# Eight semaphores instead of four for a stream of scatters, and a constant column in place of a comparison, in a four-layer graph kernel

## The reference, cut to what matters

```python
x = _layernorm(x + _L0(x, src, dst))                     # message: x[src]
x = _layernorm(x + _L1(x, edge_attr_32, W, ...))         # message: relu(x[src] + edge_attr), then two linear maps
x = _layernorm(x + _L2(x, src, dst, edge_weight, W))     # gathers x[dst] * weight, sums by src
x = _layernorm(x + _L3(x, edge_index, w_src, w_tgt, b))  # gathers x[src] * gate * norm, sums by dst
# in _L3:
deg = jax.ops.segment_sum(jnp.ones(E), src)              # how many edges leave each node
```

## Time and profile before

| what | value |
|---|---|
| median of three runs | 8055.8 us (8040.68 to 8060.42) |
| time of the profiled execution | 8085.47 us |
| its span, first to last instruction | 8083.7 us |
| granted TensorE clock, mean | 0.835 |
| busy: PE / DVE / ACT / POOL | 72% / 86% / 49% / 51% |
| sort and first scatters, about | 0 to 1380 us |
| first layer, about | 1390 to 2580 us |
| second layer, about | 2610 to 4803 us |
| third layer, about | 4926 to 6577 us |
| fourth layer, about | 6686 to 7948 us |

### The profile page before, as it was taken

How to read it: one execution, slowest core, us unless ns; L and a number is a source line. 1 busy time by engine, 2 the same in 40 slices (tenths; PEclk the granted TensorE clock), 3 DMA queues, 4 the chain that set the end, 5 groups by cost and what they waited for, 6 DMA issues and landing times. The chain is left out here.

```text
span 8083.7 us, 287895 instructions
## 1 busy us (share of the span) xinstructions
PE 5818.8 (72%) x120824; PEld 5437.1 (67%) x120824; DVE 6912.9 (86%) x8082; ACT 3967.8 (49%) x5752; POOL 4145.9 (51%) x3710
## 2 busy tenths in 40 slices
PE   5767775888885666666653255777777749999995
PEld 4666664777775666666653255777777749999995
DVE  8999998999996999998974347889889888999994
ACT  2333332444442555555542226889999853333331
POOL 4555777777777777777777730000000005666662
PEclk8888887999997888888776666777778769999996
DMA  7866212777773777777764324666666626666661
GB/s 127 148 119 119 42 27 59 174 175 175 175 175 95 210 207 205 208 209 205 210 173 120 91 78 158 204 207 212 213 209 216 203 99 215 201 204 201 202 202 43
DMA packets 1123439, 1316.76 MB, mean 163 GB/s; under 512 B 581317, under 2 KB 869253, under 8 KB 1122183
## 3 DMA queue, kind: packets, MB, share of 16 engines
q1 hardware_dynamic: 768861, 739.56, 33.3%
q10 hardware_dynamic: 250536, 508.89, 22.0%
q0 software_dynamic: 103168, 54.68, 2.8%
HBM read 902.26 MB, written 400.43 MB: 161 GB/s over the span
## 5 line engine op out<-in xcount | busy, mean ns | idle before, releaser
L675 POOL DMA_INDIRECT slot_table<-recs,idx_now x3224 | 3280.9, 1018 | 1349.9 <-issue 879.0
L1547 PE MATMUL banks<-hot_d,msg 128*96 128x256 bf16 x10192 | 1547.4, 307 | 1044.5 <-DVE msg L1032 836.2
L1547 PEld LDWEIGHTS banks<-hot_d,msg 128*96 128x96 bf16 x10192 | 1262.2, 136 | 1185.3 <-DVE msg L1032 874.0
L686 POOL TENSOR_TENSOR msg_z<-left,msg_z 128x448 bf16<-128x448 f32 x364 | 816.7, 2244 | 2387.6 <-ACT msg_z L1389 2387.6
L950 DVE TENSOR_TENSOR hot_d<-lodl,banks 128x2560 bf16<-128x2560 bf16 (+1 forms) x884 | 1487.6, 1683 | 0.0
L1356 ACT CAST far_now<-hot_td 128x3584 fp8e4<-128x3584 bf16 x364 | 1154.7, 3172 | 34.7 <-DVE hot_td L969 33.3
L1320 ACT CAST near_now<-hot_t 128x1792 fp8e4<-128x1792 bf16 x364 | 613.9, 1686 | 1035.5 <-DMA source_marks<-near_now 596.2
L1601 PE MATMUL banks<-x_win,hot_td 128*128 128x32 bf16 x30576 | 883.4, 182 | 222.9 <-issue 208.5
L1601 PEld LDWEIGHTS banks<-x_win,hot_td 128*128 128x128 bf16 x30576 | 831.6, 100 | 249.0 <-issue 234.4
L1289 ACT CAST msg<-banks 128x480 bf16<-128x480 f32 (+1 forms) x1040 | 522.1, 554 | 631.5 <-PE banks L1547 593.6
L961 DVE TENSOR_TENSOR hot_t<-lo_bc,banks 128x1280 bf16<-128x1280 bf16 (+1 forms) x884 | 807.9, 914 | 10.1 <-DMA lo_bc<-row_table 10.0
(11 more groups left out here) (190 smaller groups left out, 9974.9 us busy)
## 6 DMA issues: line engine op xcount, KB each, us to landing
lo_bc<-row_table ACTq DMA_DIRECT2D x364, 448.0 KB
dl_bc<-row_table SPq DMA_DIRECT2D x364, 448.0 KB, 4.6
target_marks<-far_now SPq DMA_DIRECT2D x364, 448.0 KB, 3.1
dl_bc<-target_marks SPq DMA_DIRECT2D x364, 448.0 KB, 4.2
lo_bc<-row_table ACTq DMA_DIRECT2D x468, 320.0 KB
slot_table<-zeros SPq DMA_DIRECT2D x52, 1617.0 KB, 10.8
rec_in<-slot_table ACTq DMA_DIRECT2D x364, 231.0 KB
source_marks<-near_now ACTq DMA_DIRECT2D x364, 224.0 KB
```

The source lines that it names most:

```text
L675: pool.indirect_dma_start(out=slot_dram[c.number], out_offset=bass.IndirectOffsetOnAxis(ap=idx_now[:, c.slot, g:g + 1], axis=0), in_=recs[ ...
L686: pool.tensor_tensor(msg3[:, blk.slot, :, 2 * D:3 * D], left3[:, blk.slot], msg3[:, blk.slot, :, D:2 * D], ALU.subtract).then_inc(msg_made ...
L1547: mm = t.matmul(banks[0:3 * D, 6 + blk.par, 0:WIN], rows[:, blk.slot, g, :], hot[:, blk.slot, g // 2, :, g % 2], start=(blk.b == 0 and g = ...
```

## The change

`LANES` goes from 4 to 8. By it there are eight semaphores `scattered[k]`; a scatter waits for the one eight places before it; `landed` counts each semaphore's share of the 62; `wait_scattered` waits on eight; and the condition at L673, `g - (LANES - 1) in (16, 32, 48)`, holds at places 23, 39 and 55 instead of 19, 35 and 51.

In the third layer column 32 of `msg_z` is set to 1.0 once, in both slots, at the start of `sum_targets`, with a drain behind it. The comparison of L1073 goes, and PE waits for one increment of `hot_d_made[2]` per block, not two.

```diff
-LANES = 4
+LANES = 8
@@ in sum_targets, on DVE
+                v.memset(msg_z[:, :, :, D], 1.0)
+                dve.drain()
                 first = Block(0, 0)
                 make_hot_td(2, first)
@@ in make_hot_s, on DVE
                                 ).then_inc(hot_d_made[2], 1)
-                v.tensor_scalar(msg_z[:, blk.slot, :, D],
-                                lodl[:, bass.ds(blk.chunk, 1), HB + blk.h0:HB + blk.h0 + BG].rearrange(
-                                    "p c g -> p (c g)"), 0.5, None, ALU.is_ge).then_inc(hot_d_made[2], 1)
@@ in sum_targets, on PE
-                    pe.wait_ge(hot_d_made[2], 2 * blk.number + 2)
+                    pe.wait_ge(hot_d_made[2], blk.number + 1)
                     pe.wait_ge(msg_made[2], blk.number + 1)
```

## The result

The changed kernel takes 7748.8 us (median of 4 runs, 7745.6 to 7758.0) against 8055.8 us: a ratio of 0.9624, 95% interval 0.9607 to 0.9641, or 307 us less. The forecast was 7750 us. The profiled execution took 7748.5 us, its span is 7746.7 us. It lies on the median of its kernel, where that of before lay 30 us above its own; so the two traces differ by 337 us and the medians by 307 us. Where those 30 us were I can't say.

What follows compares the result with a forecast made beforehand. POOL's scatter stream was taken to bound the second layer's end; 314 - 5 + 10 = 319 us off gave 7766 us for the profiled execution, 7737 us from the median, so 7750 us, range 7705 to 7870 us.

Steps and rivals of the forecast that it cites:

- ACT's waits for the stream: Second layer: ACT waits for scatters before its cast, 8 times, 374.4 us, once per chunk for the last 8 chunks.
- POOL's gain: Scatter stream: of 463.6 us of waits 347.5 us go; last scatter starts at 4403 us instead of 4739.8.
- The 11 us of longer scatters: POOL: some 160 more scatters fall into the sort, each 0.07 us longer, a loss of 11 us.
- Rival 2: Scatters before 900 us: the DMA queue limits them, those waits all stay; 7921 us, chance 0.08.
- My 10 to 11 us: Scatters before 900 us: time a late scatter takes to land, nearly covered by eight in flight, 10.2 us.
- What is late next: End of second layer: its own pace binds, 23 us to spare; last product at 4486 us, a gain of 314 us.
- a sign of being wrong: Second layer's last chunks: if ACT still waits for scatters there, the prediction is wrong.
- My 0.7 us gained per block: End of second layer: steps without scatters beside them gain 0.7 us each, 13 us for 18 steps, taken as cancelled.
- Four more waits on ACT: Second layer: `wait_scattered` has four more waits, 51 times on ACT; costs 0 to 12 us, taken as 5 us.
- The third layer: Dropping DVE's comparison saves at most 29 us; the share of blocks where PE waits, 126 of 330, arrives: 10 us.
- the 15 us for the profiled execution: Whole time: profiled execution lay 29.7 us above the median; forecast of 7750 us set between 7766 and 7737 us.
- rival 4: POOL: scatter instructions themselves take longer with eight in flight; time about 8450 us if one in four took 1.9 us, chance 0.04.

Runs made afterwards that it cites:

- lanes8: Kernel before with eight semaphores instead of four, comparison per block kept; on a chip with the long sort: 11351.6 us, ratio to before 0.9962.
- late4: Kernel before with the constant column, four semaphores, and POOL starting scatters only when all 52 chunks are ranked: 9357.1 us, ratio 1.1437.
- late8: Kernel before with the constant column, eight semaphores, and POOL starting scatters only when all 52 chunks are ranked: 9144.6 us, ratio 1.1192.

## Why the prediction was right

- **What bounds it.** ACT's waits for the stream in the earlier trace rows were read rightly but for one: of the 8 waits and 374.4 us, 39.9 us stand before the layer's first cast, at 2614 us. It is there with 39.7 us in the changed kernel and with 40.0 us in lanes8, where the scatters had long ended, so it isn't a wait for them. Seven chunks waited, 334 us. The sum doesn't use this number. The last product came 60.4 us after the last scatter, as it was 59.6 us before, and 60 us in both late kernels. That the waits for scatters pass to the time one for one while the second layer waits is shown by late4 and late8.
- **POOL's gain.** Expected: 347.5 us less 11, last scatter at 4403 us. Measured 4413.2 us, 10 us later. The waits that stay are 62.9 - 89 x 0.30 = 36 us; I had taken none. Two terms, 27 us together, made up for most of it. The 11 us of longer scatters did not come: all 3224 are busy for 3280.9 us before and 3281.4 us after. And the idle time beyond 0.30 us that the view puts down to issue fell by 16 us, from 879.0 - 2813 x 0.30 = 35 to 944.5 - 3085 x 0.30 = 19 us; nothing in my sum held that.
- **Rival 2 and the rule behind it.** Refuted wherever it was measured. Before 900 us the waits fell from 257.3 to 54.1 us, and on the other chips from over 300 to 86 to 101 us with eight and to 12 to 40 us with ten. The Trainium skill ("DMA: Bandwidth & Descriptors", Queues, rings and completion order) says that an engine drains one packet of about 9 to 17 descriptors from a queue before it turns to the next. That more in flight gain nothing was my step from it, and these runs don't bear it out. More in flight do not make a scatter land later at worst, either: from its start to the end of the wait for it, it took up to 13.1 us with four and up to 13.8 us with eight in the traces of before and after, and up to 14.3 and 14.2 us on the other chips. The longest with four (before, timeline of POOL; the second waits for the first):

```profile
814.40 2.48 POOL L675 DMA_INDIRECT slot_table<-recs,idx_now  x1 [0.30 <-issue]
...
827.52 0.96 POOL L675 DMA_INDIRECT slot_table<-recs,idx_now  x1 [6.83 <-DMA slot_table<-recs,idx_now]
```

  The longest with eight (the changed kernel, chain of work, start and duration):

```profile
642.08 13.52 DMA slot_table<-recs,idx_now
```

  My 10 to 11 us, read from one wait of the earlier trace rows, was too short: the longest wait in the same trace is 6.8 us, not 5.5. Landings of up to 13 us against a cover of 10.2 us, and of 7.6 us at a chunk's border, are why 36 us of waits stayed. Ten in flight cover 12.7 us within a chunk.
- **What is late next.** I said the layer's own pace, with 23 us to spare. The layer ran a little faster than I let it (5.07, not 5.12 us a block up to 4204 us, and 4.9 after it) and the scatters ended 10 us later, so at the very last chunk they still bound it, by about 12 us. That ACT would still wait there I had named as a sign of being wrong; it came for one chunk of seven. The last product came at 4474 us, not 4486: three blocks fewer were left at 4204 us, the rest went faster, and the wait took half of that back. So the step that put the layer's own pace last failed by a hair; pace and stream end within 12 us of each other. My 0.7 us gained per block without scatters was read from the layer's last blocks, which are short anyway; over a whole layer without scatters it is 0.3 us, on other chips.
- **Four more waits on ACT.** I put 5 us, 12 at most; the pace didn't fall, so they can't be seen.
- **The third layer.** This is the step whose mechanism failed. I let a share of 126 blocks in 330 of DVE's 0.08 us arrive, and such a share is not there: with four comparisons per block more the layer is not longer. Whether the column brought a few us in another way, through PE's wait for the comparison, is open; the column alone gives 0.9993 and 0.9998, and neither interval shuts out 10 us. I took "PE waits for line 1059" for a price. In those blocks it is one of several waits that end close together, and taking 0.08 us from it lets the next one decide; that reading is argued, not shown. The 12 us by which the layer was shorter in the changed kernel's trace look like my 10 us, but they are less than the 37 us by which this layer differs between the traces with a constant column, and that trace has the highest clock of all, 0.79.
- **The sum.** 319 us, where the traces differ by 337 and the medians by 307. I had put half of the profiled execution's 30 us on the scatters; the median gain is 12 us below the sum. That the forecast is within 2 us of the median is partly luck: the 10 us for the third layer have no support in the runs, the second layer gave 12 us more than its 314, and the 15 us for the profiled execution were a guess. One slip changes nothing: in rival 4 the mean is 1.24 us and the last scatter near 5115 us, not 5145.

## What to carry to other kernels

A ring of semaphores (or buffers) for a stream of small DMAs should cover the landing time at its worst, not its median: here 1.27 us of issue time each, and landings of up to 13 us while tables were zeroed, so eight left 36 us of waits and four 348. It should also be counted where the stream's loop starts anew: 62 places on ten semaphores leave two in flight at each chunk's border, and nearly all waits that ten semaphores left stand there. Such a stream off the critical path decides a later stage as soon as that stage catches it up, and then its waits count one for one (204 us of stream, 204 us of layer in late4 and late8); as soon as it doesn't, or something else feeds it late, little or none does, as with the long sort. A wait in the trace says which instruction was last, not what shortening it is worth: adding the same work fourfold is a cheap way to ask.

## What the runs showed that I had not expected

- The same program takes 11375 to 11400 us on three chips and 8056 and 8177 us on two others, with the difference in the sort, where PE stands idle for 2 to 3 ms with no cause in the profile. The ten traces end this sort between 5010 and 5127 us, and by kernel: 5010 to 5054 us with eight semaphores, 5084 and 5096 with four, 5093 to 5127 with ten.
- Scatters of 17 KB each, 3% of the DMA engines' time, that run beside the second layer seem to make it some 100 us longer (1848 against 1727 to 1741 us, on different chips). Nothing in my sum held such a term. Finishing the scatters before that layer begins may be worth more than a ninth or tenth semaphore; it wasn't tried.
- A faster stream can run into its own inputs: SP issues the records behind the zeroing, and in late8 POOL waits 240.7 us for them.
